# Token choice layer: rescaling shared among the expert steps, x stored ahead of the gather, selections ahead of combinations

## What is computed

```python
logits = jnp.einsum('...btd,des->...btes', grouped, controller)
logits = logits + tie
perm = (logits == jnp.max(logits, axis=-3, keepdims=True)).astype(x.dtype)
sel = jnp.einsum('...btd,...btes->...besd', grouped, perm)
inner = jax.nn.relu(jnp.einsum('...besd,desf->...besf', sel, f1) + bias)
inter = jnp.einsum('...besf,esfd->...besd', inner, f2)
out = jnp.einsum('...besd,...btes->...btd', inter, perm)
...
x = _layernorm(x + _L0_ffn_ref(x, L0_ffn_controller, L0_ffn_f1, L0_ffn_f2, L0_ffn_bias), axis=-1)
```

## Time and profile before

| | us |
|---|---|
| median of three runs (2817.12 to 2829.66) | 2828.81 |
| the profiled execution, time | 2827.45 |
| its span on the core | 2825.5 |
| PE busy in the span | 2333.9 |
| DVE busy | 1485.1 |
| ACT busy | 895.3 |
| POOL busy | 640.0 |

### The profile page before, as it was taken

The page is one execution under the profiler, slowest core; times in us unless marked ns, Lnnn a source line. Parts: engine busy times, 40 slices in busy tenths (PEclk is TensorE's granted clock), DMA queues, the critical chain, the costliest instruction groups (busy, mean ns, idle before and its releaser), DMA issues. The chain is left out here.

```text
span 2825.5 us, 44730 instructions
## 1 busy us (share of the span) xinstructions
PE 2333.9 (83%) x18544; PEld 1439.7 (51%) x18544; DVE 1485.1 (53%) x2631; ACT 895.3 (32%) x1273; POOL 640.0 (23%) x372
## 2 busy tenths in 40 slices
PE   3899999999999985768774789883688989889996
PEld 1454555555555554656563366553455555555553
DVE  1445555555555543455553166456656666665662
ACT  0233333333333333434441222120233334333332
POOL 4122112222211201121221333342103203211212
PEclk7899999999999997989897899996799999989997
DMA  6555665555566504675675111002444245225220
GB/s 137 102 106 110 118 114 111 107 112 113 109 117 115 104 17 151 224 262 201 226 260 183 51 60 60 30 30 76 134 130 134 72 115 159 80 81 160 92 84 16
DMA packets 226968, 329.18 MB, mean 117 GB/s; under 512 B 14688, under 2 KB 164560, under 8 KB 226512
## 3 DMA queue, kind: packets, MB, share of 16 engines
q1 hardware_dynamic: 223952, 325.68, 43.4%
q10 hardware_dynamic: 2816, 0.65, 0.2%
HBM read 197.71 MB, written 127.93 MB: 115 GB/s over the span
## 5 line engine op out<-in xcount | busy, mean ns | idle before, releaser
L1666 ACT ACTIVATE l1f_probs<-l1f_slot 128x1024 f32<-128x1024 f32 x240 | 241.4, 1022 | 435.3 <-PE l1f_slot L1839 355.0
L518 DVE TENSOR_REDUCE l0a_rowmax<-l0a_slot 128x4 f32<-128x1024 f32 (+1 forms) x256 | 293.4, 1156 | 127.1 <-PE l0a_slot L631 124.2
L461 ACT ACTIVATE l0a_probs<-l0a_slot 128x1024 f32<-128x1024 f32 (+1 forms) x256 | 248.4, 971 | 337.1 <-PE l0a_slot L621 189.1
L1729 DVE TENSOR_REDUCE l1f_rowmax<-l1f_slot 128x1 f32<-128x1024 f32 x240 | 287.7, 1219 | 102.2 <-PE l1f_slot L1825 102.0
L1839 PE MATMUL l1f_slot<-l1f_Qs,l1f_Ks 128*128 128x256 f32 x960 | 188.1, 324 | 38.4 <-DVE l1f_rowmax L1729 17.0
L1839 PEld LDWEIGHTS l1f_slot<-l1f_Qs,l1f_Ks 128*128 128x128 f32 x960 | 145.1, 205 | 109.0 <-DVE l1f_rowmax L1729 30.9
L1825 PE MATMUL l1f_slot<-l1f_Ks,l1f_Qs 96*128 96x512 f32 x480 | 173.5, 456 | 26.9 <-DMA l1f_Qs<-kq_rows 15.2
L621 PE MATMUL l0a_slot<-l0a_mask,l0a_ident 128*128 128x512 bf16 (+1 forms) x512 | 150.3, 376 | 25.2 <-issue 22.9
L1784 PE MATMUL l1f_os<-l1f_probs,l1f_V 128*32 128x256 f32 x1920 | 166.2, 399 | 1.8 <-ACT l1f_probs L1666 0.9
L421 POOL TENSOR_TENSOR l0a_turned<-l0a_turned 128x512 f32<-128x512 f32 x32 | 40.7, 1272 | 559.7 <-DVE l0a_turned L504 559.7
L563 PE MATMUL l0a_O<-l0a_probs,l0a_V 128*32 128x128 f32 x3840 | 156.5, 279 | 10.1 <-issue 10.1
(11 more groups left out here) (188 smaller groups left out, 4060.0 us busy)
## 6 DMA issues: line engine op xcount, KB each, us to landing
expert_outputs<-l0f_wide SPq DMA_DIRECT2D x64, 512.0 KB, 4.0
l0f_wide<-expert_outputs SPq DMA_DIRECT2D x32, 1024.0 KB, 9.6
l0a_Qs<-qk_rows SPq DMA_DIRECT2D x96, 256.0 KB, 7.8
l0a_Ks<-qk_rows SPq DMA_DIRECT2D x96, 256.0 KB, 14.9
l1f_Ks<-kq_rows SPq DMA_DIRECT2D x48, 512.0 KB, 6.8
l0f_f<-in_dram SPq DMA_DIRECT2D x10, 2048.0 KB, 15.4
qk_rows<-l0a_hi SPq DMA_DIRECT2D x32, 512.0 KB, 2.8
qk_rows<-l0a_lo SPq DMA_DIRECT2D x32, 512.0 KB, 4.2
```

The lines of the kernel that those rows point to most:

```text
L461: exp_ready.by(act.activation(probs[:, t % 2, HG * g:HG * g + HG, 0:reach, :], s[:, :, 0:reach, :], ACT.Exp, scale=SCALE))
L518: max_ready.by(dve.reduce_max(rowmax[:, t, :, 2 * g:2 * g + 2], s[:, :, :, first:2 * P], AX))
L1666: exp_done.by(act.activation(probs[:, half, u - FIRST[i], :], s[:, :], ACT.Exp, scale=SCALE))
L1729: max_done.by(dve.reduce_max(rowmax[:, 2 * u + t:2 * u + t + 1], s[:, :], AX))
```

## The change

What the edit does, by place in the list:

- **Rescaling.** `aggregate` stands behind h 0 of the first half's experts (before: behind h 1), and VectorE's four `rescale` steps (two tiles each) stand between the `inter` steps of that half (before: between the second half's first selections). GpSimd still rescales tiles 0 to 7. In the last block VectorE rescales 14 tiles and GpSimd two.
- **Transfers.** `store` 1 and `store` 0 of the block before stand ahead of `gather` 0; load, load and f2 stand behind it as before.
- **Combinations.** Of the late ones the last, out 7, stands behind all eight selections (before: sel 7 was behind it). Of the early ones the first stands behind seven selections (before: five). out 3 stands ahead of logits (before: behind).
- **Choices.** The first two pT of each half's selection stand between the last `inter` steps of the half before.
- **lo.** For the first half of the first block VectorE computes `lo`; `lo_ready` is one semaphore for each half.

```diff
@@ -688,12 +688,15 @@
         return [(offset, "out", NC * half + n) for n in range(NC)]
 
     s, e, late = selection(0), experts(0), combination(-1, 1)
-    steps = [(-1, "gather", 1), (0, "f2", 0)] + s[:10] + merged(s[10:], late) + [(0, "spread", 1)]
-    steps += e[:4] + [(-1, "aggregate", 0)] + e[4:] + [(0, "gather", 0)]
+    turned = selection(1)[:2]
+    steps = [(-1, "gather", 1), (0, "f2", 0)] + s[2:11] + merged(s[11:], late[:3]) + [late[3], (0, "spread", 1)]
+    steps += e[:1] + [(-1, "aggregate", 0)] + e[1:5] + [(-1, "rescale", 0), e[5], (-1, "rescale", 1), e[6], (-1, "rescale", 2), e[7],
+                                                        (-1, "rescale", 3), turned[0], e[8], turned[1], e[9]]
+    steps += [(-1, "store", 1), (-1, "store", 0), (0, "gather", 0), (1, "load", 0), (1, "load", 1), (0, "f2", 1)]
     s, e, early = selection(1), experts(1), combination(0, 0)
-    steps += merged(s[:10], [(-1, "rescale", n) for n in range(4)] + [(-1, "store", 0), (-1, "store", 1), (1, "load", 0), (1, "load", 1), (0, "f2", 1)])
-    steps += merged(s[10:], early[:2]) + [(1, "xT", 0), (1, "xT", 1), early[2], (1, "xT", 2), (1, "xT", 3), (1, "logits", 0), early[3]]
-    steps += [(1, "spread", 0)] + e[:4] + [(1, "second", 0)] + e[4:6] + [(1, "hi", 0), (1, "lo", 0)] + e[6:8] + [(1, "hi", 1), (1, "lo", 1)] + e[8:]
+    steps += s[2:14] + merged(s[14:], early[:1]) + [early[1], (1, "xT", 0), (1, "xT", 1), early[2], (1, "xT", 2), (1, "xT", 3), early[3]]
+    steps += [(1, "logits", 0), (1, "spread", 0)] + e[:4] + [(1, "second", 0)] + e[4:6] + [(1, "hi", 0), (1, "lo", 0)] + e[6:8]
+    steps += [(1, "hi", 1), (1, "lo", 1), (1, "pT", 0), e[8], (1, "pT", 1), e[9]]
     slotted = ("xT", "logits", "pT", "sel", "h", "inter", "out")
 
     with ExitStack() as ctx:
...
@@ -756,10 +759,15 @@
         def hidden_free(eng, X, p):
             schedule.wait_filled(eng, X if p >= 8 else X - 1, ("inter", (p - 8) // 2 % (2 * IN)))
 
-        def rescale(eng, X, n, tiles):
+        def low(eng, X, n):
+            part = slice(NT * n, NT * n + NT)
+            hi_ready.wait(eng, X, n + 1)
+            lo_ready[n].by(eng.tensor_tensor(lo[:, part, :], x[:, X % 2, part, :], words(hi[:, part, :]), ALU.subtract))
+
+        def rescale(eng, X, tiles):
             wait_alone(eng, ln.rstd_ready, ln.count(X, 0))
             for t in tiles:
-                normed[n].by(eng.tensor_scalar(x[:, X % 2, t, :], x[:, X % 2, t, :], ln.mv[:, t, 0:1], ln.rstd[:, t:t + 1],
+                normed[t // NT].by(eng.tensor_scalar(x[:, X % 2, t, :], x[:, X % 2, t, :], ln.mv[:, t, 0:1], ln.rstd[:, t:t + 1],
                                                ALU.subtract, ALU.mult))
 
         @block.sync
...
@@ -808,21 +816,20 @@
 
         @block.gpsimd
         def _(pool):
-            for s in (lo_ready, spread_ready[1], normed[0]):
+            for s in (lo_ready[1], spread_ready[1], normed[0]):
                 s.start(pool)
             pool.wait_ge(setup, NSETUP)
 
             def piece(step, X, seq, n, B):
                 _, kind, i = step
-                if kind == "lo":
-                    part = slice(NT * i, NT * i + NT)
-                    hi_ready.wait(pool, X, i + 1)
-                    lo_ready.by(pool.tensor_tensor(lo[:, part, :], x[:, X % 2, part, :], words(hi[:, part, :]), ALU.subtract))
+                if kind == "lo" and (X or i):
+                    low(pool, X, i)
                 if (kind, i) == ("spread", 1):
                     choice_ready.wait(pool, X)
                     schedule.wait_filled(pool, X - 1, ("out", 2 * NC - 1))
                     alone(pool)
-                    lo_ready.wait(pool, X)
+                    for ready in lo_ready:
+                        ready.wait(pool, X)
                     for j in range(J):
                         rows = slice(EH * j, EH * j + EH)
                         alone(pool)
...
@@ -847,7 +854,7 @@
 
             def take_choice(X, i):
                 schedule.wait_filled(act, X if i >= 2 else X - 1, ("sel", (i - 2) % (2 * TP)))
-                s = arrived(act, X, (0, "pT", i))[:, 0:2 * P].rearrange("p (t n) -> p t n", t=2)
+                s = arrived(act, X, schedule.by_name["pT", i])[:, 0:2 * P].rearrange("p (t n) -> p t n", t=2)
                 for q in range(2):
                     rows = slice(64 * q, 64 * q + 64)
                     chosen_ready.by(act.copy(chosen[rows, i % 2, :, q, :], s[rows, :, :]))
...
@@ -928,7 +935,9 @@
                 if kind == "aggregate":
                     ln.aggregate(dve, X, 0)
                 if kind == "rescale":
-                    rescale(dve, X, 1, range(NT + 2 * i, NT + 2 * i + 2))
+                    rescale(dve, X, range(NT + 2 * i, NT + 2 * i + 2) if X + 1 < NB else ((2, 3, 4), (5, 6, 7), (8, 9, 10, 11), (12, 13, 14, 15))[i])
+                if kind == "lo" and X == 0 and i == 0:
+                    low(dve, X, 0)
                 if kind == "sel":
                     tp = i % TP
                     s = arrived(dve, X, step)[:, 512:1024].rearrange("p (g e) -> p e g", e=EH)
...
@@ -987,7 +997,7 @@
                 if kind == "sel":
                     chosen_ready.wait(pe, X, 2 * i + 2)
                     if i < TP and i % (TP // 2) == 0:
-                        lo_ready.wait(pe, X, 2 * i // TP + 1)
+                        lo_ready[2 * i // TP].wait(pe, X)
                 if kind == "h" and i % 2 == 0:
                     pe.wait_ge(f1_loaded, 16 * CH)
                     sel_even.wait(pe, X, TP * (i // 2 + 1))
```

More of the change, by code:

```diff
@@ L729, in token_choice_layer @@
         xT_even = signal("xT_even", CH); xT_odd = signal("xT_odd", CH)
-        hi_ready = signal("hi_ready", 2); lo_ready = signal("lo_ready", 2)
+        hi_ready = signal("hi_ready", 2); lo_ready = [signal(f"lo_ready{n}", 1) for n in range(2)]
         rated = signal("rated", 2); best_ready = signal("best_ready", 2); choice_ready = signal("choice_ready", 2)
@@ L837, in piece @@
                     ln.reciprocal_root(pool, X, 0)
-                    rescale(pool, X, 0, range(NT))
+                    rescale(pool, X, range(NT) if X + 1 < NB else range(2))
             schedule.loop(pool, piece)
@@ L898, in _ @@
         def _(dve):
-            for s in (xT_odd, rated, best_ready, choice_ready, normed[1], sel_odd, hidden_odd, inter_odd, summed):
+            for s in (xT_odd, rated, best_ready, choice_ready, lo_ready[0], normed[1], sel_odd, hidden_odd, inter_odd, summed):
                 s.start(dve)
@@ L953, in piece @@
                     if i == 0:
-                        lo_ready.wait(dve, X)
+                        for ready in lo_ready:
+                            ready.wait(dve, X)
                     if i >= NC:
```

## The result

The changed kernel takes **2800.4 us**, the median of six executions (2794.75 to 2808.3); the kernel before, on the same chip, 2829.23 us (2817.12 to 2834.16). The ratio of the means is 0.9904, with a 95% interval of 0.9879 to 0.9929: 1% faster, 29 us by the medians, and the new median is 2.4 us above the forecast of 2798. The profiled execution took 2808.3 us with a span of 2806.1.

What follows compares the result with a forecast made beforehand. TensorE's waits, for gathers, the load of x and lo, were taken as what can be won. Terms of 12.0 + 9.6 + 3.9 - 1.2 + 2.1 + 3.9 = 30.3 us gave 2798 us, range 2786 to 2811.

Steps and rivals of the forecast that it cites:

- Stores ahead of the gather, 12.0 us: Second halves of blocks 1 and 2, and block 3: stores fill the transfer hole, load lands 4.0 us earlier; 12.0 us won.
- Rescaling among the experts, 0: First half's experts: VectorE's last copy ends 2.2 us later, but queued inter transfers cover it; gather's release unmoved, 0 us.
- GpSimd, 0: SP's queue at store 0: GpSimd's eight tiles are done 5.4 us before the gather's issue, so 0 us.
- Last late combination behind the selections, 9.6 us: End of the selections: h follows out 7 without waiting for a copy; 3.5 us, in block 1 2.6, together 9.6 us won.
- out 3 ahead of logits, 3.9 us: Blocks 0 to 2: out 3 fills the 1.36 us wait ahead of logits; 1.3 us each, 3.9 us won.
- The choices, -1.2 us: First two pT among the experts: ScalarE's copies delay its last inter copies; 0.4 us in three blocks, 1.2 us lost.
- lo of the first half, 2.1 us: First half block: VectorE computes lo instead of GpSimd, so selections start near 1104.0; 2.1 us won.
- The end, 3.9 us: End of the layer: VectorE's fourteen tiles take 6.0 us where GpSimd's took 9.90; 3.9 us won.
- (1): Rival: VectorE's tiles take as long as GpSimd's and make the gather late, 4.7 us lost three times; 2812 us, chance 0.13.
- (2): Rival: the load comes no earlier, the hole stays and 12.0 us fall away; 2810 us, chance 0.10.
- (3): Rival: SP's queue stops at store 0, everything behind waits for GpSimd's eighth tile; 2843 us, chance 0.03.
- (4): Rival: the clock stays up for xT and stores hide wholly, 2 to 3 us more per block; 2790 us, chance 0.14.

Runs made afterwards that it cites:

- Experiment 1: Changed kernel with the gather issued ahead of the two stores again: 2814.55 us, ratio 0.9950 to the kernel before.
- experiment 8: Changed kernel with VectorE's eight rescaled tiles of each block but the last cut to 4 of 256 columns: 2803.18 us, ratio 0.9911 to the kernel before.
- Experiment 6: Changed kernel with the four late combinations mixed with the last selections as before: 2808.11 us, ratio 0.9936 to the kernel before.
- 3: Changed kernel with the next block's first two pT behind the second half's last inter again: 2804.97 us, ratio 0.9909 to the kernel before.
- 10: Changed kernel with GpSimd computing both lo of the first block and the last block's tiles split eight and eight: 2808.91 us, ratio 0.9935 to the kernel before.
- 2: Changed kernel with spread 0 moved behind the first h of the second half's experts: 2799.89 us, ratio 0.9898 to the kernel before.
- experiment 4: Changed kernel with spread 0 behind h 0 and the next block's first two pT behind the last inter: 2799.69 us, ratio 0.9895 to the kernel before.
- experiment 7: Changed kernel with logits ahead of out 3 again: 2801.34 us, ratio 0.9907 to the kernel before.
- 11: Changed kernel with logits ahead of out 3 and the next block's first two pT behind the last inter: 2794.54 us, ratio 0.9889 to the kernel before.
- experiment 5: Changed kernel measured and traced once more, unchanged: 2803.83 us, ratio 0.9917 to the kernel before.

## Why the prediction was right, and where it was not

**Stores ahead of the gather, 12.0 us: right.** Experiment 1 gives back 11 to 14, some 3 of them by its own second hole. xT comes 3.0 us earlier after h in the rows shown and 3.4 in the mean of blocks 1 and 2 over both pairs of traces, not 4.0; block 3, where the 3.26 us wait for f2 is gone, is 4.9 shorter where 4.0 stood. Together that is 11.7, though no run takes block 3's part apart. The prediction said that the wait ahead of out 0 would fall to 4 us; it is 6.4. The later gather was charged with its bytes (2.3 us); its first piece lands 3.6 us later after its issue and 2.9 later after h. That wait costs little, as the prediction argued, since TensorE then waits for x in any case.

**Rescaling among the experts, 0: right,** by experiment 8; and **GpSimd, 0: right,** with 4.4 us between its eighth tile and the gather where 5.4 were reckoned (store 0's issue, 1.4 us, lies in them). On the rule weighed in the prediction: eight tiles of VectorE between 1341 and 1346 us took 0.40 to 0.58 us each; GpSimd's took 1.23 to 1.33 us beside them and 1.22 alone. So GpSimd is a little slower beside a busy VectorE, by up to 0.1 us a tile. The prediction had it as no slower, but in the kernel before, too, it took 1.22 to 1.36 us against 1.21 or 1.22. The Trainium skill, SBUF — State Buffer, section "SBUF: two separate sides", would have one block the other for a whole instruction; the trace of the changed kernel does not show it either: no tile waits for a whole one of the other engine.

**Last late combination behind the selections, 9.6 us: right in kind.** Experiment 6 gives 7.4, and h follows out 7 with 0.6 us of waiting, for the last selection's copy.

**out 3 ahead of logits, 3.9 us: this is the step that failed.** The prediction saw that out 3 fills the 1.36 us wait ahead of logits, and that much came: logits has no wait. It did not ask what out 3 had covered where it stood. Behind logits come VectorE's marks, ScalarE's spread 0 and only then the relu of h 0. With out 3 between logits and h TensorE waited 0.78 us for that relu, without it 2.44: 1.7 us in each of three blocks. That moves every later inter of the half and their gather. Over the 21 blocks profiled with spread 0 ahead of the relu and no out 3 there (the changed kernel twice, experiments 1, 3, 6, 8, 10), the gather is issued 26.98 us after h on average, over the other 18 (the kernel before twice, 2, 4, 7, 11) 24.57. Of these 2.4 us, 1.7 are the wait itself. Another 0.3 come from four of the 21 blocks in which the clock fell behind the wait, as here:

```profile
1392.77 2.46 PE L1049 MATMUL l0f_slot<-l0f_f,l0f_hidden 64*128 64x256 f32 x16 [2.44 <-ACT l0f_hidden L896]
```

The first inter takes 2.4 to 2.6 us instead of 2.0 in them and the last copy comes 1.6 us later still; behind a wait of 0.78 us this happened in none of the 18. The last 0.4 us are late landings (see the last section), which were commoner in these traces; that the delay makes them so is not shown. Among the kernels with the turned order of the late combinations, the first halves take 45.6 us on average with the delay and 43.8 (experiments 2, 4, 7, 11) without it: 1.9 us each, 5.5 in all, lost to the move. With experiment 7 the term is worth nothing that can be told: the layer is 2.1 us shorter without the move, and between experiments 3 and 11, which differ by the same move, 2.7 us longer. The gain and the loss cancel within the scatter.

**Rest of the first halves.** Without that loss they take 43.8 us; the terms gave 43.1 (45.9 - 2.8; among its signs the prediction named 42). One part is in the traces: in these twelve blocks the first late combination takes 2.9 us on average, in the six of the kernel before 2.5, since more of them run at the lower clock. In the block of the changed kernel shown above it is 3.68 us behind a wait of 3.56, where it was 1.95 behind 1.69.

**The choices, -1.2 us: small, as forecast.** The trace of the changed kernel made me suspect them, since the last copy comes 3.3 us later after h. But half of that is spread 0. For the rest, the gather is issued 0.3 us earlier in experiment 4 than in 2 and 0.6 us later in 11 than in 7, two pairs that differ by the choices alone. No run tells the 0.4 us a block of the prediction from nothing.

**lo of the first half, 2.1 us: right.** The wait ahead of the first selection falls from 5.50 to 3.36 us, and what ends it now is ScalarE's copy of the first choice, as the prediction had it. The start as a whole is 3.7 us shorter. The selections behind it are about 1 us quicker when lo is not GpSimd's, for which the traces name no cause, and the rest is scatter.

**The end, 3.9 us: right in size, wrong in cause.** The tail shortened by 4.6, but VectorE's fourteen tiles give only 1.4 of it; 3.2 come from the order of the stores, which the prediction did not count at the end. Fourteen tiles took 5.14 us, from 1525.28, but then both stores go out together at 1530.50, and the next layer begins 7.9 us after that.

Sum: the layer is 23 us shorter in the means of two traces, where 30.3 were forecast; the whole kernel is 29 shorter by its medians. The forecast's median was so near partly by luck. The layer fell 7 us short, and the layer of an unchanged kernel moves by 3 to 7 us between two traces; the second measurement of the same two kernels (experiment 5) gives 0.9917, or 23 us. The four rivals stand as follows. VectorE did not make the gather late (1). The load did come earlier (2). SP did not stop at store 0 (3). Of more than the sum (4) one part came in places: xT took 3.46 instead of 3.68 us in the rows shown, and 3.49 to 3.68 in the other three such blocks of the changed kernel.

## What to carry to other kernels

A wait that an operation can fill is half of the reckoning; the other half is what that operation covers where it stands now. Before moving it, read the chain behind it on the other engines (here marks, spread, relu), and price the wait that appears. And where a queue of dependent transfers alternates with holes, put transfers that nobody waits for soon into the hole; here that was the largest term.

## What the runs showed of the hardware

**A landing has two values.** The gather leaves when all eight inter transfers have landed. In the 18 blocks without the delay it was issued 24.0 to 24.4 us after h in 13 and 25.3 to 25.8 in 5; in the 21 with it, 25.7 to 26.0 in 6 and 27.0 to 28.9 in 15. Windows of the changed kernel in a late case, its gather issued at 1307.69:

```profile
1297.40:1304.90 7.50, 5.53 (x32) 4.61 (x33) 3.10 (x5) 5.96 (x12) 7.50 (x2) 0.81 0.94 371
1305.70:1307.20 1.50, 1.50 (x14) 1.32 (x12) 0.87 (x2) 1.30 (x4) 0.65 (x1) 1.00 0.10 38
```

When the flow has ended, 38 GB/s trickle on for 1.5 us, a tenth of the full rate, and only then is the gather released. The single packets in the trace show what trickles: from 1305.87 to 1307.12 a packet of 4096 bytes starts every 0.16 us, one at a time, and the last completion stands at 1307.27, when the others have been there for 1.3 us. So one of the 16 DMA engines ends late. The packets also show what the late cases share. Between 9 us after h and the gather each of the 39 blocks has one transfer of 16 KB of program code (the packet's kind is "instruction"), 0.9 to 1.7 us long. The last six inters flow almost without a pause, from about 16 us after h on without the delay, 17.4 with it, and 19 in four blocks whose copies were late:

| blocks | the code transfer starts | us after h | the last completion comes behind the 14th of 16 by, us |
|---|---|---|---|
| 22 | ahead of that flow | 11.0 to 17.2 | 0.0 to 0.1 |
| 17 | within it | 17.4 to 23.3 | 1.0 to 1.7 |

These 17 are among the 20 late blocks; in the other three the copies themselves were 1.6 us late. So a code transfer within the flow goes with one engine that ends late. That it is the same engine is the obvious reading, but a packet does not name its engine. The hole of the kernel before, from which the prediction starts, is such a case too: code at 1352.08, the last completion 1.6 us behind, so that about half of the 3 us hole was this. No run moved the code transfer, and why it falls into the flow in 12 of the 21 blocks with the delay and in 5 of the 18 without stays open. The Trainium skill, DMA: Bandwidth & Descriptors, section "Why a DMA increments its semaphore by 16 and not by 1", says that the engines finish independently and that only the full count means that all has landed. The completions of this trace agree: the gather leaves 0.4 to 0.6 us after the last of them, in late cases too.

**A longer wait is paid twice.** The granted clock was 0.50 from 1313.41 to 1317.02, behind the 3.56 us wait, in the changed kernel, and 1.00 at the same place of the kernel before, behind 1.69 us:

```profile
1313.41:1317.02 3.61, 3.61 (x17) 1.71 (x17) 0.00 (x0) 0.00 (x0) 0.00 (x0) 0.50 1.09 355
```

```profile
1314.50:1316.40 1.90, 1.89 (x17) 1.07 (x17) 0.00 (x0) 0.00 (x0) 0.00 (x0) 1.00 1.06 356
```

That is 1.2 against 2.4 GHz, and 3.68 against 1.95 us for the same sixteen matmuls. So this late gather costs some 1.7 us (3.68 - 1.95) more than its lateness. It is not quite a matter of the wait alone: in block 1 of the kernel before, the same combination took 3.25 us behind a wait of 1.82, and in experiment 1 another took 1.95 behind 2.27.
